# A fused two-layer feed-forward kernel on one core: moving one hi/lo split ahead of a counting step, three down products behind a later up product, and the order round the first and last down tiles

## The reference

```
x = x + layernorm(A(layernorm(x)));  x = x + layernorm(F(layernorm(x)))      # x: 4 x 512 x 512, float32
A(x): s = silu(x @ w_gate.T)                     # 2048 tokens x 1376
      set to 0 the 688 values of smallest |s| of each token
      return (s * (x @ w_up.T)) @ w_down.T
F(x): return (silu(x @ W_gate.T) * (x @ W_up.T)) @ W_down.T
```

## Time and profile before

| | |
|---|---|
| median of 3 runs | 719.76 us (719.27 to 720.15) |
| the profiled execution | 720.74 us, of which the span of the core 718.9 us |
| PE busy | 706.9 us (98%) |
| DVE busy | 582.4 us (81%) |
| ACT busy | 383.1 us (53%) |
| POOL busy | 248.4 us (35%) |

### The profile page before, as it was taken

One profiled execution on the slowest core, in us unless ns is written; L12 is line 12 of the kernel. 1 busy time (PEld: TensorE's weight loads), 2 busy tenths in 40 slices (PEclk: granted clock), 3 DMA queues, 4 the chain that ended last, 5 costly groups with the idle time before them and its releaser, 6 DMA issues.

```text
span 718.9 us, 9847 instructions
## 1 busy us (share of the span) xinstructions
PE 706.9 (98%) x3181; PEld 594.8 (83%) x3181; DVE 582.4 (81%) x1013; ACT 383.1 (53%) x610; POOL 248.4 (35%) x377
## 2 busy tenths in 40 slices
PE   8999999999999999999999999999999999999997
PEld 7888878888888888888888887877887888877885
DVE  6789778888898888987789889998688988877443
ACT  5896577677677566776654335433354333323230
POOL 1423123332323323233232666613315665621001
PEclk9999999999999999999999999999999999999999
DMA  8641424223554435544332677244953533334341
GB/s 276 200 110 63 100 70 98 56 78 87 124 130 83 100 86 116 128 84 111 102 107 72 174 232 217 87 156 115 247 143 111 161 119 111 93 111 147 137 142 44
DMA packets 126214, 88.56 MB, mean 123 GB/s; under 512 B 66416, under 2 KB 106608, under 8 KB 126160
## 3 DMA queue, kind: packets, MB, share of 16 engines
q1 hardware_dynamic: 126160, 87.91, 45.0%
HBM read 49.87 MB, written 18.87 MB: 96 GB/s over the span
## 4 chain that ended last, share of the span: by engine, by line
PE 68%; DVE 11%; issue 8%; ACT 5%; POOL 4%; DMA 3%; SPq 1%; DVEq 0%; ACTq 0%; POOLq 0%
PE gu_ps L813 14%; PE y_ps L754 13%; PE gu_ps L740 11%; PE tr_ps L813 10%; PE tr_ps L740 8%; PE gu_ps L835 4%; PE tr_ps L835 3%; ACT junk L937 3%; POOL move L1795 2%; PE gu_ps L788 2%; PE tr_ps L788 2%; PE y_ps L835 1%; DVE below L1376 1%; POOL thr L1798 1%; DVE xstat L1247 1%
## 5 line engine op out<-in xcount | busy, mean ns | idle before, releaser
L937 ACT ACTIVATE junk<-absv,thr 128x1383 bf16<-128x1383 f32 x96 | 139.1, 1449 | 43.4 <-POOL thr L1798 42.5
L754 PE MATMUL y_ps<-down_hi,hT 128*128 128x512 f32 x352 | 109.1, 391 | 0.0
L1795 POOL TENSOR_SCALAR move<-sgn 128x1 f32<-128x1 f32 x80 | 41.8, 522 | 108.0 <-ACT junk L937 108.0
L754 PEld LDWEIGHTS y_ps<-down_hi,hT 128*128 128x128 f32 x352 | 66.1, 188 | 14.4
L754 PE MATMUL y_ps<-down_lo,hT 128*128 128x512 f32 x176 | 69.5, 395 | 2.2 <-DVE hT L1279 2.2
L740 PE MATMUL gu_ps<-gate_hi,xT 128*128 128x460 f32 (+1 forms) x232 | 67.7, 373 | 0.0
L740 PE MATMUL gu_ps<-up_hi,xT 128*128 128x460 f32 (+1 forms) x232 | 67.2, 371 | 0.0
L1777 POOL TENSOR_TENSOR yrstd<-yvar,half 128x1 f32<-128x1 f32 x32 | 23.5, 736 | 85.3 <-DVE yvar L1288 85.3
L1770 POOL TENSOR_TENSOR xrstd<-xvar,half 128x1 f32<-128x1 f32 x32 | 21.9, 685 | 77.1 <-DVE xvar L1251 77.1
L1818 POOL TENSOR_TENSOR prod<-prod,gate_lo_raw 128x512 f32<-128x512 f32 (+1 forms) x20 | 26.1, 1305 | 64.3 <-DVE prod L1509 64.3
L740 PEld LDWEIGHTS gu_ps<-gate_hi,xT 128*128 128x128 f32 x232 | 44.1, 190 | 5.0
(11 more groups left out here) (306 smaller groups left out, 1923.2 us busy)
## 6 DMA issues: line engine op xcount, KB each, us to landing
absv<-prod SPq DMA_DIRECT2D x64, 176.0 KB, 3.4
h_scratch<-prod SPq DMA_DIRECT2D x38, 256.0 KB, 2.8
xin<-x_scratch SPq DMA_DIRECT2D x18, 256.0 KB, 2.7
xres<-in_L_attn_x SPq DMA_DIRECT2D x16, 256.0 KB, 3.4
x_scratch<-xres SPq DMA_DIRECT2D x16, 256.0 KB, 2.5
xg_even<-xin SPq DMA_DIRECT2D x64, 64.0 KB, 2.6
up_lo<-h_scratch SPq DMA_DIRECT2D x8, 512.0 KB, 3.8
up_hi<-h_scratch SPq DMA_DIRECT2D x8, 512.0 KB, 4.4
```

The source lines that it names most:

```text
L754: last = nc.tensor.matmul(y_ps[:, :], h, w[:, c, :], start=(c == 0 and i == 0), stop=(c == JC - 1 and i == 2))
L937: nc.scalar.activation(junk[:, 0:I + PAD], absv[:, q, A0 - PAD:A0 + I], ACT.Sign, bias=thr[:, q:q + 1], scale=-1.0, accum_out=sgn[:, q:q + ...
L1795: stepped(nc.gpsimd.tensor_scalar(move[:, :], sgn[:, q:q + 1], sgn[:, q:q + 1], float((WINDOW - 1) ** 2) + 0.5, ALU.mult, ALU.is_gt))
```

## The change

- On the third tile (tile 2) ACT makes `split_h_hi(2)` in turn 3, between `normalise_y(1)` and `count(3,4)`; it was at the head of turn 4, behind `count(3,4)`. DVE makes `split_h_lo(2)` ahead of `find_below(3)`; it was behind it.
- PE's down products: `down(3)` moves behind U(5,2), `down(4)` behind U(6,1), `down(5)` behind U(7,1). The others stay.
- `last_h_hi` and `last_h_lo` take half 1 before half 0; tiles of half 0 then wait for both halves, tiles of half 1 for one.
- In the last unit of the first pass `x_normalise` goes behind the first two parts of `tile_lo(0, ..)`.
- At the end of the first pass `y_stats` of the last tile goes ahead of four steps on DVE (two `right_lo`, one `add_residual`, `right_lo` of operand 4), and `add_residual` of the last tile ahead of `right_lo` of operand 7.
- `keep_busy` before the first transposes issues 19 in place of 15, the one behind them 9 in place of 10.

```
+    SOON = range(4, 5)
...
-                pe.wait_ge(lasth_lo, 2 * g + half + 1)
+                pe.wait_ge(lasth_lo, 2 * g + 2 - half)
...
-            keep_busy(15)
+            keep_busy(19)
             transpose_x(0)
-            keep_busy(10)
+            keep_busy(9)
...
                 for n in range(3):
                     product(j, 1, n)
-                    if n == max(6 - j, 0) and j < TILES - 1:
+                    if n == max((9 - j) // 2, 0) and j < TILES - 1:
                         down(j - 2)
...
             for j in range(3, TILES - 1):
-                if 3 < j < LATE:
+                if 3 < j < LATE and j not in SOON:
                     split_h_hi(j - 2)
...
                 normalise_y(j - 2)
+                if j + 1 in SOON:
+                    split_h_hi(j - 1)
                 count(j, 4)
...
+            last_h_hi(0, 1)
             last_h_hi(0, 0)
-            last_h_hi(0, 1)
...
-                dve.wait_ge(lasth_hi, 2 * g + half + 1)
+                dve.wait_ge(lasth_hi, 2 * g + 2 - half)
...
+                if j in SOON:
+                    split_h_lo(j - 2)
                 find_below(j - 1)
-                if 3 < j < LATE:
+                if 3 < j < LATE and j not in SOON:
                     split_h_lo(j - 2)
...
                 sum_u4(u)
-                if u in XU:
-                    x_normalise(XU[u])
                 if u == JC - 1:
                     tile_lo(0, 0)
                     tile_lo(0, 1)
+                if u in XU:
+                    x_normalise(XU[u])
                 gate1(u)
...
+            last_h_lo(0, 1)
             last_h_lo(0, 0)
-            last_h_lo(0, 1)
...
-                y_stats(TILES + r)
+                if r < S_TILES - 1:
+                    y_stats(TILES + r)
                 for a in XD.get(r, ()):
                     x_normalise(a)
                 for i in SUM_AT.get(r, ()):
                     right_sum(1, i)
+                if r == S_TILES - 2:
+                    y_stats(TILES + r + 1)
                 for i in R_AT.get(r, ()):
+                    if i == TSEQ[-1]:
+                        add_residual(TILES + r)
                     right_lo(1, i)
-                add_residual(TILES + r)
+                if r < S_TILES - 1:
+                    add_residual(TILES + r)
```

More of the change, by code:

```diff
@@ L1202, in _ @@
             tile_hi(S_TILES, 2)
+            last_h_hi(1, 1)
             last_h_hi(1, 0)
-            last_h_hi(1, 1)
             tile_hi(S_TILES + 1, 0)
@@ L1734, in _ @@
                 h0(u)
+            last_h_lo(1, 1)
             last_h_lo(1, 0)
-            last_h_lo(1, 1)
             tile_lo(S_TILES + 1, 0)
```

## The result

| | before | after |
|---|---|---|
| median of 20 runs each | 719.85 us (719.01 to 720.96) | 720.67 us (719.76 to 723.58) |
| ratio, 95% interval | | 1.0014 [1.0008, 1.0021] |
| profiled execution (span) | 720.74 us (718.9) | 723.58 us (721.8) |

The account below looks back on a forecast made before the run. PE, busy 706.9 of 718.9 us, was taken as the bound, so only its gaps could close. Terms -0.1 + 0.65 + 0.72 + 0.1 = 1.4 us took 719.76 to 718.4; range for 8 in 10: 716.9 to 719.5.

Parts of the forecast that it names:

- The third tile's split: At down(2): removes PE's 1.23 us wait, while ACT stands 1.6 us and the threshold search becomes 1.4 us late.
- All before PE asks for them by my reading: Steps queued on ACT behind the waiting split come 1.4 us or more late, yet still before PE needs them.
- The later down products: First layer: moving down(3) to down(5) gives h 2.5 us each, leaving PE 1.1 us ahead behind down(4).
- The end of the first layer: Near 363 us: 0.3 us of search lateness passes silu(15,2), against 0.2 spare at right_lo(0,0); first layer's term -0.1 us.
- PE is late there, whatever it won before: At PE's use of right_lo(0,0), 363.22 us: PE is 0.1 us late regardless of its earlier gain.
- Round the first down tiles: End of the first layer, near 485 to 494 us: PE's second tile starts 0.65 us earlier, 0.37 of it included.
- The last down tile: Near 556 us: earlier y_stats removes PE's whole 0.72 us wait; bounds 0 to 0.72.
- The new last step is `right_lo(1,7)`: Near 555 us on DVE: this step now ends the row, 0.4 us ahead of PE.
- The start: Before the first x transposes: four more warming transposes fill a 0.94 us gap; worth 0.1 us, bounds 0 to 0.5.
- The early gain passes: Rival: search under 1.1 us late at tile 15, PE keeps 0.5 to 1.1; 717.1 us, chance 0.25.
- The tail gains half: Rival: POOL's two steps run slow again or right_lo(1,7) ends late; 719.1 us, chance 0.2.
- The slower rival: First layer: late count(3,4) shifts POOL's steps under select, search 4.2 us late, deciding from about 2.8; 721.2 us, chance 0.07.

Follow-up runs that it names:

- the tail alone: Before with only the changes round the first and last down tiles (last_h orders, x_normalise, y_stats and add_residual moved): 720.00 us, ratio 0.9999.
- the kernel with the warming products alone: Before with only 19 in place of 15 warming transposes ahead of the first x transposes and 9 in place of 10 behind: 720.13 us, ratio 0.9996.
- The first layer's part alone: Before with only tile 2's split ahead of the count and down(3), down(4), down(5) later: 721.35 us, ratio 1.0018.

## Why the prediction was wrong, point by point

- **The third tile's split: right in itself.** Predicted: wait of 1.6 on ACT (1.62), `find_below(3)` at 103.35 (103.68), search 1.4 late (1.87, 1.54 without the start's shift).
- **"All before PE asks for them by my reading": the step that failed.** It was said of what is queued behind the waiting split, and `split_x_hi(5)` was named. That one has time. But the same kind of step at x tile 8 had only 0.87 us, less than the lateness of 1.4 that I had just worked out, and it would have been short even with PE at its old time. I had looked at every place where PE waited before, and at h and the end of the layer; not at the operand that changes its place in the order at turn 7. The term was -0.1; four profiles say -1.0, and with the clock's fall -2.7. The other kernels bear it out: with one split moved, 1.13 us come back in the first layer's part, and with the third tile's split at its old place and x tile 8's split moved the kernel gains.
- **The later down products: right.** Waits of 0.7 and 0.2 at `down(3)` and `down(4)` were left, the gain behind `down(4)` is real, and 0.4 to 0.8 us with the search on time.
- **The end of the first layer: not reached, and read too narrowly.** With PE late nothing waits at 363. With PE 1.0 early nothing waits either, since silu(15,2) takes the search along. "PE is late there, whatever it won before" treated the search as fixed; what counts is its lateness plus PE's lead against 1.13.
- **Round the first down tiles: +0.65 predicted, 0.4 measured.** The size was wrong. PE's wait at the second tile fell from 0.90 to about 0.64, as predicted. From `down(15)` to tile 1 the nine profiles with the turned order take 94.21 us on average (93.68 to 94.53), the nine without 94.61 (94.29 to 95.03). The two los of the last h do follow their his without a gap, but `x_normalise` now stands in front of the last unit's sums. In the tail alone it comes late itself, because POOL's step for it took 2.17 us, against 0.55 in before (the first line of the second fence under the next point). It takes 2.17 in all three kernels with the tail and the old warming products, and there PE waits another 0.28 to 0.33 us for the last h; with the tail and the 19 and 9 products it takes 1.01 in all six profiles, though DVE does the same two-input subtractions beside it. What makes the difference is open. The tail alone:

```profile
482.16 2.17 POOL L1782 TENSOR_TENSOR xrstd<-xvar,half 128x1 f32<-128x1 f32 x1 [3.25 <-DVE xvar L1255]
...
484.37 0.55 DVE L1260 TENSOR_SCALAR xin<-xin,xmv,xrstd 128x512 f32<-128x512 f32 x1 [0.45 <-POOL xrstd L1782]
...
491.68 0.50 PE L846 MATMUL y_ps<-down_lo,xT 96*128 96x512 f32 x1 [0.28 <-DVE xT L1533]
...
493.29 0.47 PE L837 MATMUL gu_ps<-down_lo,h_two 128*128 128x512 f32 x1 [0.63 <-DVE h_two L1541]
```

- **The last down tile: +0.72 predicted, -0.4 measured.** (From tile 1 to the last tile 212.04 us on average with the change and 211.66 without; single profiles spread by over 1 us, so the size is rough.) The wait at 556 is gone in all nine profiles with the change, but for 0.16 us in one. But it was not a fixed 0.72 in the kernels without it: 0 to 1.0, 0.3 on average, and no wait in four of nine. So the step of the prediction that failed here is the size of the wait, read from one execution. And there is a later cost that I did not follow. "The new last step is `right_lo(1,7)`": the load of the next left operand waits for just this step. Counted from the start of the second pass's first unit on PE, it is issued at 7.4 us on average, against 6.5 in the nine profiles without the change, and POOL starts on it 4.2 to 5.0 us later, against 3.5 to 3.6 in eight of those nine. So POOL's sums, ACT's hi and DVE's lo come later: the lo ends at 19.3 on average against 16.9, and PE asks for it at 19.1. PE loses up to 0.7 us there, and some tenths more at the next products. Why the load takes longer is open; the kernel with the warming products alone has it too (4.4). After:

```profile
562.09 0.74 POOL L1819 TENSOR_TENSOR stage<-stage 128x256 f32<-128x256 f32 x1 [8.17 <-DMA stage<-in_L_ffn_W_up]
...
565.58 1.70 ACT L1008 ACTIVATE xg_even<-stage 128x1792 fp32r<-128x1792 f32 x1 [4.68 <-POOL stage L1824]
...
567.32 2.03 DVE L1436 TENSOR_TENSOR xg_even<-stage,xg_even 128x1792 fp32r<-128x1792 f32 x1 [3.94 <-ACT xg_even L1008]
...
569.40 0.50 PE L815 MATMUL gu_ps<-up_hi,xg_even 128*128 128x512 f32 x1 [0.26 <-DVE xg_even L1436]
```

and before, with the `x_normalise` step of POOL ahead of it:

```profile
482.75 0.55 POOL L1770 TENSOR_TENSOR xrstd<-xvar,half 128x1 f32<-128x1 f32 x1 [3.24 <-DVE xvar L1251]
...
557.68 0.74 POOL L1807 TENSOR_TENSOR stage<-stage 128x256 f32<-128x256 f32 x1 [3.41 <-DMA stage<-in_L_ffn_W_up]
...
560.73 1.71 ACT L1006 ACTIVATE xg_even<-stage 128x1792 fp32r<-128x1792 f32 x1 [1.24 <-POOL stage L1812]
...
562.47 2.03 DVE L1432 TENSOR_TENSOR xg_even<-stage,xg_even 128x1792 fp32r<-128x1792 f32 x1
```

- **The start: +0.1 predicted, nothing measured.** `down(0)` starts at 58.32 on average over seven profiles with 19 and 9 products and at 58.30 over eleven with 15 and 10. The rows give a granted clock of 1.00 from the first microsecond on, in all these profiles, so the level has to be read from the lengths. With 15 products, the four x transposes behind them take 1.11 or 1.12 us in eight profiles and 0.66 in three; with 19, from 0.66 to 1.11. Where they take 0.66, nothing but transposes came ahead. The rule that the prediction took from the Trainium skill (TensorE: Matmul & The Clock Gate, PE-mode transpose), that a transpose does not count as busy for the clock as a matmul does, does not fit these lengths. The first layer's part alone is such a case, to be held against the earlier trace rows:

```profile
6.07 0.66 PE L724 MATMUL tr_ps<-ident,xin 128*128 128x128 f32 x4 [0.95 <-DVE xin L1260]
```

  So by the lengths the clock's rise falls before or behind these transposes by chance, in both kernels. With 15 products `down(0)` starts at 57.93, 57.95 and 58.45 in the three quick cases and at 58.23 to 58.55 in the eight others: up to 0.5 us earlier, but not each time.
- **The sum.** Predicted +1.4, with -0.1 for the first layer, +1.37 for the tail, +0.1 for the start. Measured by the table: -1.0 (the fall of the clock left out), 0.0 (0.4 gained to tile 1, 0.4 lost behind it), 0.0. That makes 719.85 + 1.0 = 720.85, and the median is 720.67.
- **The rivals.** "The early gain passes" did not come, since PE's gain was lost at tile 8. "The tail gains half" came out as a tail that gains nothing, by a mechanism that it did not name. The slower rival had the right sign and the wrong cause: POOL's slow steps shifted with `select`, as was said against it; in the first layer there are as many of them in after as in before, at the same turns. The point from which the search's lateness hurts was not 2.8 us, as it said, but below 0.9. The rule that was weighed for POOL (GPSIMD Engine Reference, Key points, in the Trainium skill) may be behind the 2.17 us above, in a place where I had not applied it; but since the same step took 1.01 us beside the same subtractions, the runs do not settle it.

## What to carry to other kernels

When a side chain is made later by some amount, list everything that hangs on it with its spare time, tile by tile, and not only what waits now; an operand that changes its place in the order at some turn is where the spare is smallest. A wait of PE that is removed is worth what the next one leaves of it: here h, then x tile 8, then x tile 9, then h again. And a step put last in a row is the one whose own followers, here a load, start later: follow these too.

## What the runs showed of the hardware

A short stand of PE can cost twice. After a wait of 1.89 us and one of 3.19 us the granted clock was 0.50 in the next full row of 2 us above and PE lost 1.7 and 1.4 us more; after waits of 1.53, 1.64, 1.72 and 1.80 us at the same place as the first it stayed in full. Five points do not fix a bound, and whether the same length of wait would always do the same is open.
